# Splitting both products of an MLP into three one-pass products in a fused graph-transformer layer

## The chip, the cores and the metric

The kernel runs on one core of one Trainium2 chip. The metric is the device time of one execution, in microseconds (us). TensorE is called PE below, VectorE is DVE, ScalarE is ACT, GpSimd is POOL and SyncE is SP, as in the profile.

## The reference, cut to what matters

There are 6250 nodes with 512 features and 100000 edges. Three branches are computed and added up:

```python
xn = layernorm(x)
x = x + gnn(xn, edge_index, W1, b1, W2, b2) + mix(xn, ...)
x = x + ffn(layernorm(x))
# gnn: h = relu(xn @ W1 + b1) @ W2 + b2;  h + segment_sum(h[col], row)
# the end of mix:
y = v + (y @ proj_w + proj_b)
h2 = layernorm(y, n2_g, n2_b)
h2 = gelu(h2 @ mlp_w1 + mlp_b1)
h2 = h2 @ mlp_w2 + mlp_b2
return y + h2
```

The two products with `mlp_w1` and `mlp_w2` (both 512x512) are the ones that change.

## The kernel before

The 6250 rows are 125 partitions of 50 rows; a step handles two of the 50, so there are 25 steps (`STEPS`), numbered `t.u` from 0 to 24. The program has five stages, and every engine's order is written out by hand:

1. Start and first pass (`phase1`): weights are prepared, the edges are sorted on DVE, and the 256 hidden values of the gnn are stored to `hidden_rows` in HBM.
2. Second pass (`phase2`): the attention output of each step is computed and stored to `y_rows`. It has 8 edge groups in each step.
3. The mlp stage (`v` from 0 to 24 of the last loop): each step loads its `y_rows`, normalizes them on ACT (`norm_rows`, L1303), transposes them on PE (L973), multiplies by `mlp1_w` (`features`, L986, in two halves `i`), takes the gelu on ACT (`gelus`, L1331), multiplies by `mlp2_w` (`mlp2`, L995, in two halves), adds the result up on DVE (`z_rows`, L1881) and stores it to `z_rows` in HBM. It has 7 or 8 edge groups in each step, spread over it in four parts (`counts`).
4. The tail (`v` from 25 on, 3 edge groups a step while there are any left): the last branch (ffn) for each step, and the stores of the output.

Edge groups run under stages 2 to 4. There are 440 of them (`PAIRS`). A group is a pair of blocks of 128 edges. POOL issues one indirect DMA (a gather, L612) for each block, 880 in all, which brings the hidden rows of 128 edges into one place of a ring of 12 pairs (`RING`). ACT makes one-hot matrices for them (L1279, L1283), PE multiplies one by the other (L879 to L882), and DVE adds the sum to the accumulators in SBUF (`add_groups`, L1744). A gather for pair n waits until PE has used pair n - 12. PE's group n waits until both gathers of n have landed and until DVE has added group n - 2.

POOL's order in the last loop is: gathers up to a fixed number, then `roots` (L621, the inverse roots of the variances for the tail), then the next gathers. For `v` = 24 that is all gathers up to pair 405, which is gather 812, and then `roots` of step 0:

```python
gathers(TURN + sum(SECOND) + BETWEEN + sum(THIRD[:v]) + soon + RING)
if 0 <= b + 1 < STEPS:
    roots(steps[b + 1])
```

DVE's `ll_rows` (L1923) waits for these roots; behind it on DVE are the last `add_groups`, `z_rows` of step 24, and all of the tail.

SP's queue stores and loads in program order. In the mlp stage it stores `z_rows` of step v - 1, waits for that store, loads x for step v + 1, and then loads `y_rows` for step v + 2.

An f32 matmul is recorded as two matmuls by the profiler. Products with operands of type F32R are recorded as one each (L904 to L906 in `phase2`, for example), and so are those of 16 bit operands (L879 to L882).

## Time and profile before

| what | value |
| --- | --- |
| time, 3 runs | 1731.53 us median (1728.9 to 1735.38) |
| the profiled execution's own time | 1733.09 us |
| its span, first to last instruction | 1731.3 us |
| PE busy | 1598.6 us (92%) |
| DVE busy | 1044.2 us (60%) |
| ACT busy | 809.6 us (47%) |
| POOL busy | 1038.0 us (60%) |
| mean granted TensorE clock | 0.969 of full speed |

The profile gives each engine's busy time and, for each group of instructions, the idle time ahead of it and what ended that idle time. A share of busy time is an average over stages that have different limits, and it counts neither the sequencer's work between two instructions nor the waits. The second pass lasts from about 500 to 1012 us, the mlp stage from there to about 1480 us, and the tail to the end.

### The profile page before, as it was taken

To read this page: it belongs to the slowest core of one execution; us is meant where nothing else is said; L and a number is where in the kernel's file an instruction comes from. 1 tells how busy PE (TensorE), PEld (TensorE's weight loads), DVE (VectorE), ACT (ScalarE), POOL (GpSimd) and SP (SyncE) were. 2 spreads that over 40 slices of the span, in tenths; PEclk is the share of its full clock that TensorE was granted. 3 is DMA by queue.
4 is the path that set the end of the run, shared out by engine and by line. 5 is a ranking of instruction groups with operands and counts; after the bars stand their busy time and mean duration, and the time that the engine had idled before them with its cause. 6 is when DMAs were issued, how large, how long until landed. Compare 5 with 4: busy or idle time off the path is not lost.

```text
span 1731.3 us, 25102 instructions
## 1 busy us (share of the span) xinstructions
PE 1598.6 (92%) x8243; PEld 1241.5 (72%) x8243; DVE 1044.2 (60%) x2340; ACT 809.6 (47%) x1892; POOL 1038.0 (60%) x1131
## 2 busy tenths in 40 slices
PE   5999999998899999999999889999999999689997
PEld 3778877787677788878888656777667667467775
DVE  6899999997245555556555433333334334478896
ACT  2234444444334444445445555554654555256543
POOL 3124444343667777777777777777777777767110
PEclk9999999999899999999999889999999999899998
DMA  6023232322346556555665565666556566545332
GB/s 197 13 69 120 87 99 81 103 74 83 118 122 202 176 173 190 184 178 176 182 190 181 167 205 175 183 187 186 186 181 188 188 182 192 176 143 184 139 130 100
DMA packets 87427, 263.63 MB, mean 152 GB/s; under 512 B 18765, under 2 KB 20813, under 8 KB 87298
## 3 DMA queue, kind: packets, MB, share of 16 engines
q0 software_dynamic: 43456, 119.44, 24.7%
q1 hardware_dynamic: 43842, 142.59, 23.9%
q8 instruction: 68, 1.11, 0.3%
q14 instruction: 61, 0.50, 0.1%
HBM read 217.15 MB, written 44.80 MB: 151 GB/s over the span
## 4 chain that ended last, share of the span: by engine, by line
PE 44%; DMA 16%; DVE 15%; issue 11%; POOL 8%; ACT 5%; DVEq 0%; SPq 0%; POOLq 0%; ACTq 0%
PE bank L995 7%; DMA sb_step<-y_rows 6%; DVE sb_weights L1464 6%; DMA z_rows<-sb_step 5%; POOL sb_weights L612 4%; PE bank L934 3%; PE bank L986 3%; PE bank L904 2%; PE bank L906 2%; PE bank L905 2%; DMA sb_step<-x_t 2%; PE turn_bank L880 2%; PE bank L880 2%; DMA sb_weights<-hidden_rows,sb_weights 2%; DVE sb_step L1645 2%
## 5 line engine op out<-in xcount | busy, mean ns | idle before, releaser
L612 POOL DMA_INDIRECT sb_weights<-hidden_rows,sb_weights x880 | 862.6, 980 | 291.1 <-issue 246.1
L1279 ACT ACTIVATE sb_weights<-sb_const,sb_weights 128x125 f16<-128x125 f16 x880 | 266.9, 393 | 46.7 <-PE turn_bank L882 46.7
L1744 DVE TENSOR_TENSOR sb_acc<-sb_acc,bank 125x257 f32 x220 | 92.4, 420 | 301.4 <-PE bank L882 256.8
L995 PE MATMUL bank<-sb_weights,sb_step 128*125 128x512 f32 x400 | 181.6, 597 | 2.3 <-ACT sb_step L1402 2.3
L986 PE MATMUL bank<-sb_weights,sb_step 128*128 128x250 f32 x800 | 179.2, 377 | 0.0
L1744 DVE TENSOR_TENSOR sb_acc<-sb_acc,turn_bank 125x257 f32 x220 | 92.3, 419 | 143.5 <-PE turn_bank L882 125.1
L1464 DVE TENSOR_TENSOR sb_weights<-sb_weights 128x512 f32<-128x512 f32 (+3 forms) x256 | 164.3, 683 | 3.6
L986 PEld LDWEIGHTS bank<-sb_weights,sb_step 128*128 128x128 f32 x800 | 149.5, 192 | 15.8
L579 POOL TENSOR_SCALAR sb_const<-sb_const 125x2 f32<-125x2 f32 x25 | 10.0, 402 | 239.8 <-ACT sb_step L1181 239.8
L1197 ACT ACTIVATE sb_step<-sb_step 125x256 f32<-125x256 f32 x100 | 48.1, 502 | 214.0 <-DVE sb_step L1637 213.4
L728 PE MATMUL bank<-sb_w_parts,sb_x_high 128*125 128x512 f32 (+1 forms) x400 | 139.3, 348 | 0.0
L729 PE MATMUL bank<-sb_w_parts,sb_x_high 128*125 128x512 f32 (+1 forms) x400 | 135.3, 338 | 0.0
L730 PE MATMUL bank<-sb_w_parts,sb_x_low 128*125 128x512 f32 (+1 forms) x400 | 135.1, 338 | 0.0
L995 PEld LDWEIGHTS bank<-sb_weights,sb_step 128*125 128x125 f32 x400 | 71.7, 189 | 76.3 <-issue 73.7
L1283 ACT ACTIVATE sb_weights<-sb_weights,sb_const 128x1000 f16<-128x1000 f16 x110 | 124.1, 1129 | 3.6
L1303 ACT ACTIVATE sb_step<-sb_step,sb_const 125x512 f32<-125x512 f32 x50 | 37.9, 805 | 182.6 <-DMA sb_step<-y_rows 181.8
L741 PE MATMUL bank<-sb_w_parts,sb_x_high 128*125 128x256 f32 (+1 forms) x300 | 102.5, 342 | 16.3 <-DVE sb_step L1645 13.6
L1317 ACT COPY sb_step<-bank 128x500 f32<-128x500 f32 x25 | 14.4, 576 | 192.5 <-PE bank L922 192.5
L934 PE MATMUL bank<-sb_const,sb_step 128*125 128x512 f32 x200 | 95.3, 599 | 0.0
L743 PE MATMUL bank<-sb_w_parts,sb_x_low 128*125 128x256 f32 (+1 forms) x300 | 94.6, 315 | 0.0
L742 PE MATMUL bank<-sb_w_parts,sb_x_high 128*125 128x256 f32 (+1 forms) x300 | 94.5, 315 | 0.0
L835 PE MATMUL bank<-sb_step 125*128 125x256 f32 x400 | 90.8, 380 | 1.1 <-ACT sb_step L1257 1.1
(314 smaller groups left out, 3654.5 us busy)
## 6 DMA issues: line engine op xcount, KB each, us to landing
sb_step<-x SPq DMA_DIRECT2D x63, 500.0 KB
sb_step<-x_t SPq DMA_DIRECT2D x50, 500.0 KB, 6.8
sb_weights<-hidden_rows,sb_weights POOLq DMA_INDIRECT x880, 4.6
y_rows<-sb_step SPq DMA_DIRECT2D x25, 500.0 KB
sb_step<-y_rows SPq DMA_DIRECT2D x25, 500.0 KB
z_rows<-sb_step SPq DMA_DIRECT2D x25, 500.0 KB
sb_step<-z_rows SPq DMA_DIRECT2D x13, 500.0 KB
out<-sb_step SPq DMA_DIRECT2D x13, 500.0 KB
```

The costliest lines, as they stand in the source:

```text
L612: pool.indirect_dma_start(out=ring[:, n % RING * 2 + h, 0:HID], out_offset=None, in_=table, in_offset=bass.IndirectOffsetOnAxis(ap=row_of[ ...
L728: pe.matmul(bk, high, rhs(0, c), start=c == 0, stop=False)
L729: pe.matmul(bk, high, rhs(1, c), start=False, stop=False)
L730: mm = pe.matmul(bk, low, rhs(0, c), start=False, stop=c == KC - 1)
L741: pe.matmul(outs[c], high, first, start=c == 0, stop=False)
L934: mm = pe.matmul(banks[m][0:P, :], qpT[:, c, m * P:(m + 1) * P], pmat[:, c, :], start=False, stop=c == KH - 1)
L986: last = pe.matmul(bk[:, (c % 2) * 250:(c % 2) * 250 + 2 * P], mlp1_w[:, k, c * 128:(c + 1) * 128], hT3[:, t.s, k, :], start=k == 0, stop= ...
L995: mm = pe.matmul((BC, BD)[m][0:P, :], gT3[:, k, m * P:(m + 1) * P], mlp2_w[:, k, :], start=k == 0, stop=k == KC - 1)
L1279: mm = act.activation(hit[q % 2][:, i, :], iota_h[:, :], ACT.Abs, bias=less_lane[:, q * BP + i // 2, i % 2:i % 2 + 1])
L1283: act.activation(hit[q % 2], hit[q % 2], ACT.Relu, scale=-1.0, bias=one_c[:, 0:1]).then_inc(hits, 1)
L1464: sort_op(dve.tensor_tensor(half(target, c, lo), a, b, op))
L1744: dve.tensor_tensor(dst, dst, (BE, BH)[n % 2][0:P, 0:RW], ALU.add).then_inc(g_add, 1)
```

## The change

`features` gets its weights and its activations as two f16 parts each. The weights are scaled by a power of two for each output column, and the gelu's `scale` on ACT takes the power back. `mlp2` gets both operands as two F32R parts. Each product then becomes high x high, high x low and low x high, three matmuls of one pass. What goes with it:

- In the second pass, DVE and PE find the columns' squared norms (`mlp1_square_rows` behind step 4, `mlp1_norms` and `mlp1_scales` behind step 5), turn the powers into a column per output (`mlp1_columns`, `mlp1_scaled` behind step 6) and split the weights (`mlp1_halves` behind step 7).
- The first load of `y_rows` (`load_yd(0, 0)`), which has taken place in SP's queue behind step 3, moves behind step 11.
- ACT writes the high part of the transposed rows (`copy_hT`) and DVE the low part (`hT_low`). DVE writes both parts of the gelus (`split_gelus`). `mlp2` now waits for DVE's `g_split` instead of ACT's `feat_c`.
- `mlp2_w` is split once, its high part on ACT and its low part on DVE in step 0 of the mlp stage.

```diff
+        G_WORDS, G_AT, G_HIGH_AT, W2_HIGH_AT = KC * 2 * P, 7072, 8632, 128
...
+        G_LOW = sb("gelus_low", G_WORDS)
+        sb("rows_behind_gelus", G_HIGH_AT - G_AT - G_WORDS)
+        G_HIGH = sb("gelus_high", G_WORDS)
+        sb("mlp1_place", STEP_WORDS + W2_HIGH_AT - G_HIGH_AT - G_WORDS)
+        W2_HIGH = sb("mlp2_high", KC * D)
+        sb("constants_behind", CONST_WORDS - W2_HIGH_AT - KC * D)
...
-        mlp2_w, (gnn2_w, gnn2_low), (_, gnn2_high) = same_place(KC, D)[0], same_place(KH, D), same_place(KH, D)
-        hT3, z_first = same_place(2, KC, 2 * P)[0], [same_place(2, D)[0] for _ in range(3)]
+        (mlp2_w, mlp2_low), (gnn2_w, gnn2_low), (_, gnn2_high) = same_place(KC, D), same_place(KH, D), same_place(KH, D)
+        mlp2_high = by_chunk(W2_HIGH[:, :])
+        hT_place, z_first = same_place(2 * KC * 2 * P)[0], [same_place(2, D)[0] for _ in range(3)]
+        hT3 = hT_place.bitcast(F16).rearrange("p (s h c r) -> p s h c r", s=2, h=2, c=KC)
...
+        halves_of = lambda v: [v[:, at:at + D // 2].bitcast(F16) for at in range(0, v.shape[1], D // 2)]
+        mlp1_squares = [ATT[:, RAW_WORDS + 2 * D:RAW_AT], EDGE[:, 4 * PAIRS:4 * PAIRS + D], halves[0][:, D:2 * D], halves[1][:, D:2 * D]]
+        mlp1_high = halves_of(EDGE[:, 4 * PAIRS:4 * PAIRS + 3 * D // 2]) + halves_of(mlp1_w[:, 0, :])[1:]
+        mlp1_low = [zero_row.bitcast(F16), halves_of(mlp1_w[:, 0, :])[0]] + halves_of(mlp1_w[:, 1, :])
+        mlp1_back = n2g
...
-                elif t.u == 3:
+                elif t.u == 11:
                     sp.wait_ge(r_st[0], 16 * 13 + 1)
                     sp.wait_ge(r_st[1], 16 * 12 + 1)
+                    sp.wait_ge(*made("mlp1_split"))
                     load_yd(0, 0)
...
+            def mlp1_norms():
+
+                pe.wait_ge(*made("mlp1_squares"))
+                for k in range(KC):
+                    mm = pe.matmul(BF[:, :], ones[:, :], mlp1_squares[k], start=k == 0, stop=k == KC - 1)
+                mm.then_inc(made("mlp1_norms")[0], 1)
+
+            def mlp1_columns():
+
+                pe.wait_ge(*made("mlp1_scales"))
+                for c in range(KC):
+                    mm = pe.matmul(BF[:, c:c + 1], mlp1_squares[0][0:1, c * 128:(c + 1) * 128], ones[0:1, 0:1], start=True, stop=True)
+                mm.then_inc(made("mlp1_columns")[0], 1)
...
                 if t.u == 4:
                     pe.wait_ge(ev("m1b_ok"), 1)
+                elif t.u == 6:
+                    pe.wait_ge(*made("mlp1_scales"))
+                elif t.u == 7:
+                    pe.wait_ge(*made("mlp1_columns_read"))
...
+                elif t.u == 5:
+                    mlp1_norms()
+                elif t.u == 6:
+                    mlp1_columns()
...
                     for k in range(KC):
-                        last = pe.matmul(bk[:, (c % 2) * 250:(c % 2) * 250 + 2 * P],
-                                         mlp1_w[:, k, c * 128:(c + 1) * 128], hT3[:, t.s, k, :],
-                                         start=k == 0, stop=k == KC - 1)
+                        high, low = (v[k][:, c * 128:(c + 1) * 128] for v in (mlp1_high, mlp1_low))
+                        pe.matmul(out, high, hT3[:, t.s, 0, k, :], start=k == 0, stop=False)
+                        pe.matmul(out, high, hT3[:, t.s, 1, k, :], start=False, stop=False)
+                        last = pe.matmul(out, low, hT3[:, t.s, 0, k, :], start=False, stop=k == KC - 1)
                 last.then_inc(feat, 1)
 
             def mlp2(t, i):
-                pe.wait_ge(feat_c, t.u * 2 + i + 2)
+                pe.wait_ge(g_split, t.u * 2 + i + 2)
                 for m in (0, 1):
                     for k in (2 * i, 2 * i + 1):
-                        mm = pe.matmul((BC, BD)[m][0:P, :], gT3[:, k, m * P:(m + 1) * P], mlp2_w[:, k, :],
-                                       start=k == 0, stop=k == KC - 1)
+                        high, low = (v[:, k, m * P:(m + 1) * P].bitcast(F32R) for v in (g_high, g_low))
+                        w_high, w_low = (v[:, k, :].bitcast(F32R) for v in (mlp2_high, mlp2_low))
+                        pe.matmul((BC, BD)[m][0:P, :], high, w_high, start=k == 0, stop=False)
+                        pe.matmul((BC, BD)[m][0:P, :], high, w_low, start=False, stop=False)
+                        mm = pe.matmul((BC, BD)[m][0:P, :], low, w_high, start=False, stop=k == KC - 1)
...
-            def copy_hT(t, dst):
+            def copy_hT(t):
 
                 for i, bk in ((0, BF), (1, BG)):
                     act.wait_ge(tr, t.g * 2 + i + 2)
-                    act.copy(dst[:, t.s, 2 * i:2 * i + 2, :].rearrange("p a b -> p (a b)"), bk[:, 0:500]).then_inc(h_t, 1)
+                    act.copy(hT3[:, t.s, 0, 2 * i:2 * i + 2, :].rearrange("p a b -> p (a b)"), bk[:, 0:500]).then_inc(hT_high, 1)
...
-                                        bias=m1b[:, c:c + 1])
+                                        scale=mlp1_back[:, c:c + 1], bias=m1b[:, c:c + 1])
...
             act.wait_ge(ev("m1b_ok"), 1)
+            act.wait_ge(w2m_in, 16)
+            act.wait_ge(y_read, 2 * STEPS + 1)
+            act.copy(mlp2_high.bitcast(F32R), mlp2_w).then_inc(made("mlp2_high")[0], 1)
...
+            def mlp1_square_rows():
+
+                for k in range(KC):
+                    mm = dve.tensor_tensor(mlp1_squares[k], mlp1_w[:, k, :], mlp1_w[:, k, :], ALU.mult)
+                mm.then_inc(made("mlp1_squares")[0], 1)
+
+            def mlp1_scales():
+
+                dve.wait_ge(*made("mlp1_norms"))
+                back, scale, bits, _ = (v.bitcast(I32) for v in mlp1_squares)
+                seq(dve.tensor_copy(mlp1_squares[2], BF[:, :]))
+                ts(bits, bits, 24, ALU.logical_shift_right)
+                ts(scale, bits, -1.0, ALU.mult, 203.0, ALU.add)
+                ts(bits, bits, 51.0, ALU.add)
+                ts(scale, scale, 23, ALU.logical_shift_left)
+                ts(back, bits, 23, ALU.logical_shift_left)
+                dve.drain().then_inc(made("mlp1_scales")[0], 1)
+
+            def mlp1_scaled():
+
+                dve.wait_ge(*made("mlp1_columns"))
+                dve.tensor_copy(mlp1_back[:, :], BF[:, 0:KC])
+                dve.drain().then_inc(made("mlp1_columns_read")[0], 1)
+                seq(dve.tensor_tensor(mlp1_w, mlp1_w, mlp1_squares[1].unsqueeze(1).to_broadcast([128, KC, D]), ALU.mult))
+
+            def mlp1_halves():
+
+                for k in range(KC):
+                    if k < 3:
+                        seq(dve.tensor_copy(mlp1_high[k], mlp1_w[:, k, :]))
+                    seq(dve.tensor_tensor(mlp1_low[k], mlp1_w[:, k, :], mlp1_high[k], ALU.subtract))
+                    if k == 0:
+                        seq(dve.tensor_copy(mlp1_high[3], mlp1_w[:, 3, :]))
+                dve.drain().then_inc(made("mlp1_split")[0], 1)
...
+                elif t.u == 4:
+                    mlp1_square_rows()
+                elif t.u == 5:
+                    mlp1_scales()
+                elif t.u == 6:
+                    mlp1_scaled()
+                elif t.u == 7:
+                    mlp1_halves()
...
+            def hT_low(t):
+
+                for i, bk in ((0, BF), (1, BG)):
+                    part = lambda h: hT3[:, t.s, h, 2 * i:2 * i + 2, :].rearrange("p a b -> p (a b)")
+                    dve.wait_ge(hT_high, t.g * 2 + i + 2)
+                    dve.tensor_tensor(part(1), bk[:, 0:500], part(0), ALU.subtract).then_inc(h_t, 1)
+            hT_low(each_step(0)[0])
...
+            def split_mlp2():
+
+                dve.wait_ge(*made("mlp2_high"))
+                dve.tensor_tensor(mlp2_low.bitcast(F32R), mlp2_w, mlp2_high, ALU.subtract).then_inc(made("mlp2_split")[0], 1)
+
+            def split_gelus(t, i):
+
+                part = lambda v: v[:, 2 * i:2 * i + 2, :].rearrange("p a b -> p (a b)")
+                dve.wait_ge(feat_c, t.u * 2 + i + 2)
+                seq(dve.tensor_copy(part(g_high).bitcast(F32R), part(gT3)))
+                dve.tensor_tensor(part(g_low).bitcast(F32R), part(gT3), part(g_high), ALU.subtract).then_inc(g_split, 1)
...
-                    add_groups(counts[0] + counts[1])
+                    add_groups(counts[0])
+                    if a == 0:
+                        split_mlp2()
+                    split_gelus(steps[a], 0)
+                    add_groups(counts[1])
+                    split_gelus(steps[a], 1)
+                    if a + 1 < STEPS:
+                        hT_low(steps[a + 1])
```

What stands on DVE in one step of the mlp stage. Before, from the step's addition of y and x (L1871, L1873) on, with the adds of two groups (L1744, each behind its register load, ISA):

```order
L1871 TENSOR_TENSOR sb_step<-sb_step 125x1024
L1873 TENSOR_TENSOR sb_step<-sb_step,sb_const 125x1024
L1744 ISA
L1744 TENSOR_TENSOR sb_acc<-sb_acc,bank 125x257
L1744 ISA
L1744 TENSOR_TENSOR sb_acc<-sb_acc,turn_bank 125x257
```

Now, in the changed kernel, from the second of these adds on (L1794 there):

```order
L1794 TENSOR_TENSOR sb_acc<-sb_acc,turn_bank 125x257
L1985 CAST sb_gelus_high<-sb_step 128x500
L1986 TENSOR_TENSOR sb_gelus_low<-sb_step,sb_gelus_high 128x500
L1794 ISA
L1794 TENSOR_TENSOR sb_acc<-sb_acc,bank 125x257
L1794 ISA
L1794 TENSOR_TENSOR sb_acc<-sb_acc,turn_bank 125x257
L1985 CAST sb_gelus_high<-sb_step 128x500
L1986 TENSOR_TENSOR sb_gelus_low<-sb_step,sb_gelus_high 128x500
L1948 TENSOR_TENSOR sb_weights<-bank,sb_weights 128x500
L1948 TENSOR_TENSOR sb_weights<-turn_bank,sb_weights 128x500
```

Each step gains a cast and a subtraction from SBUF for each half of the gelus, and two subtractions from PSUM for the next step's transposed rows.

What stands on DVE between step 5 and step 6 of the second pass. Before, the end of `row_stats` (L1771) and the start of the next step:

```order
L1769 BN_AGGR sb_const<-sb_const 125x2 x2
L1771 COPY sb_const<-sb_const 125x4
L1814 SCALAR_TENSOR_TENSOR sb_step<-sb_step,sb_const 125x256 x2
L1818 TENSOR_SCALAR sb_step<-sb_step 125x2
L1820 RECIPROCAL sb_step<-sb_step 125x2
```

Now, in the changed kernel, the same place (L1821 is the end of `row_stats`, L1899 the start of step 6):

```order
L1819 BN_AGGR sb_const<-sb_const 125x2 x2
L1821 COPY sb_const<-sb_const 125x4
L1869 COPY sb_step<-bank 128x512
L1473 TENSOR_SCALAR sb_step<-sb_step 128x512
L1473 TENSOR_SCALAR sb_weights<-sb_step 128x512
L1473 TENSOR_SCALAR sb_step<-sb_step 128x512
L1473 TENSOR_SCALAR sb_weights<-sb_weights 128x512
L1473 TENSOR_SCALAR sb_weights<-sb_step 128x512
L1899 SCALAR_TENSOR_TENSOR sb_step<-sb_step,sb_const 125x256 x2
```

`mlp1_scales` has come in between: a read of PSUM and five operations on 512 columns, behind a wait for PE.

What stands on PE between the same two steps. Before, the last product of y (L934), the last group and the first product of the next step (L904):

```order
L934 MATMUL bank<-sb_const,sb_step 125x512 x2
L879 MATMUL turn_bank<-sb_weights 125x257
L880 MATMUL turn_bank<-sb_weights 125x256 x2
L882 MATMUL turn_bank<-sb_weights 125x257
L904 MATMUL bank<-sb_w_parts,sb_x_high 125x512
```

Now, in the changed kernel:

```order
L972 MATMUL bank<-sb_const,sb_step 125x512 x2
L899 MATMUL turn_bank<-sb_weights 125x257
L900 MATMUL turn_bank<-sb_weights 125x256 x2
L902 MATMUL turn_bank<-sb_weights 125x257
L920 MATMUL bank<-sb_weights,sb_const 128x512 x2
L920 MATMUL bank<-sb_step,sb_const 128x512 x2
L938 MATMUL bank<-sb_w_parts,sb_x_high 125x512
```

`mlp1_norms` has come in: four f32 products of 512 columns.

## Rows read from the trace of the kernel before

**Rows 1.** Groups by line, 1012 to 1465 us: count, busy us, mean ns, idle before:

```profile
L612 POOL DMA_INDIRECT sb_weights<-hidden_rows,sb_weights x355 | 345.2, 972 | 108.2 <-issue 98.1 <-PE turn_bank L882 6.1 <-PE bank L882 4.0
L995 PE MATMUL bank<-sb_weights,sb_step 128*125 128x512 f32 x384 | 174.4, 597 | 2.3 <-ACT sb_step L1402 2.3
L986 PE MATMUL bank<-sb_weights,sb_step 128*128 128x250 f32 x768 | 172.1, 377 | 0.0
...
L1871 DVE TENSOR_TENSOR sb_step<-sb_step 125x1024 f32<-125x1024 f32 x24 | 29.4, 1227 | 3.1 <-DMA sb_step<-x 2.5 <-DVE sb_const L1862 0.2
...
L1858 DVE TENSOR_SCALAR sb_weights<-sb_weights,sb_const 128x512 f32<-128x512 f32 x2 | 0.9, 478 | 0.0
```

**Rows 2.** The chain that ended last, in order: start us, us, what:

```profile
1260.78 12.35 DMA z_rows<-sb_step
1273.53 14.31 DMA sb_step<-y_rows
1290.51 3.44 PE bank L995 x8
...
1299.68 12.34 DMA z_rows<-sb_step
```

**Rows 3.** Groups by line from the start to 607.0 us, POOL, then PE:

```profile
L612 POOL DMA_INDIRECT sb_weights<-hidden_rows,sb_weights x120 | 119.2, 994 | 50.1 <-issue 34.7 <-DMA hidden_rows<-sb_step 6.7 <-PE bank L882 6.7
L879 PE MATMUL bank<-sb_weights 128*125 128x257 f16 x25 | 7.2, 288 | 8.2 <-DMA sb_weights<-hidden_rows,sb_weights 6.5 <-DVE sb_acc L1744 1.7
```

**Rows 4.** The same from the start to 1471.2 us:

```profile
L612 POOL DMA_INDIRECT sb_weights<-hidden_rows,sb_weights x794 | 777.4, 979 | 257.1 <-issue 223.0 <-PE bank L882 14.9 <-PE turn_bank L882 12.5
L879 PE MATMUL bank<-sb_weights 128*125 128x257 f16 x196 | 54.6, 278 | 16.9 <-DMA sb_weights<-hidden_rows,sb_weights 7.2 <-issue 4.8 <-DVE sb_acc L1744 4.6
```

**Rows 5.** Timeline of POOL: start us, us, what, idle before:

```profile
607.54 0.94 POOL L612 DMA_INDIRECT sb_weights<-hidden_rows,sb_weights  x1 [1.17 <-PE bank L882]
...
627.25 0.96 POOL L612 DMA_INDIRECT sb_weights<-hidden_rows,sb_weights  x1 [0.30 <-issue]
...
646.69 1.04 POOL L612 DMA_INDIRECT sb_weights<-hidden_rows,sb_weights  x1 [0.30 <-issue]
...
1224.64 1.82 POOL L612 DMA_INDIRECT sb_weights<-hidden_rows,sb_weights  x1 [0.30 <-issue]
...
1493.60 0.95 POOL L612 DMA_INDIRECT sb_weights<-hidden_rows,sb_weights  x1 [0.30 <-issue]
1494.57 0.72 POOL L621 TENSOR_TENSOR sb_step<-sb_step,sb_const 125x2 f32<-125x2 f32 x1
```

**Rows 6.** Timeline of DVE, columns as in rows 5:

```profile
627.38 0.62 DVE L1827 TENSOR_SCALAR sb_step<-sb_step 125x256 f32<-125x256 f32 x2
...
646.55 0.62 DVE L1827 TENSOR_SCALAR sb_step<-sb_step 125x256 f32<-125x256 f32 x2
...
1224.41 1.22 DVE L1871 TENSOR_TENSOR sb_step<-sb_step 125x1024 f32<-125x1024 f32 x1
...
1495.33 0.16 DVE L1923 SCALAR_TENSOR_TENSOR sb_step<-sb_step 125x2 f32<-125x2 f32 x1 [14.25 <-POOL sb_step L621]
```

**Rows 7.** Timeline of PE, two F32R and two f16 products:

```profile
607.57 0.40 PE L906 MATMUL bank<-sb_w_parts,sb_x_low 128*125 128x512 f32 x1
607.80 0.40 PE L904 MATMUL bank<-sb_w_parts,sb_x_high 128*125 128x512 f32 x1
...
1211.21 0.27 PE L879 MATMUL bank<-sb_weights 128*125 128x257 f16 x1
1211.32 0.38 PE L880 MATMUL bank<-sb_weights 128*125 128x256 f16 x2
```

**Rows 8.** The chain that ended last, at step 4 of the second pass:

```profile
586.64 10.13 DMA sb_step<-x_t
```

**Rows 9.** DMA issues of the page, KB each, median us to landing:

```profile
sb_step<-x_t SPq DMA_DIRECT2D x50, 500.0 KB, 6.8
sb_weights<-hidden_rows,sb_weights POOLq DMA_INDIRECT x880, 4.6
```

More of the change, by code:

```diff
@@ L1367, in _ @@
             act.wait_ge(v_mm, STEPS + 1)
-            copy_hT(steps[0], hT3)
+            copy_hT(steps[0])
             one_hots(2 * STEPS + 4)
@@ L1387, in _ @@
                     if a + 1 < STEPS:
-                        copy_hT(steps[a + 1], hT3)
+                        copy_hT(steps[a + 1])
                     hits_until(ahead + sum(counts[0:2 if a == 2 else 3]))
```

34 lines of the change are left out of this document (20 added, 14 removed).

## The prediction

> **What bounds the kernel now.** I began with the chain of waits, since PE is busy for 92% of the span. In the mlp stage the chain runs through PE's products and, every two steps, through a store of z_rows (12.35 us) and a load of y_rows (14.31 us); from one such store to the next it is 1299.68 - 1260.78 = 38.9 us, 19.4 a step [rows 2]. Read alone, this says that the mlp's products set the time. So the next view is that of the groups by line in this stage, and there the row to look at is POOL's, which the chain hardly names. Of 453 us the gathers fill 345.2 us busy and 108.2 us idle, which is all of it, and the idle time is 108.2 / 355 = 0.30 us ahead of each [rows 1]. A single gather shows the same 0.30 us, named "issue" [rows 5]: that is POOL's own time between two of them, not a wait. POOL is thus full at one gather per 1.25 us or a little more (0.95 + 0.30), whatever its 60% of busy time says.
>
> Does PE wait for it? A count tells. By 1471.2 us POOL has begun 794 gathers and PE 196 + 196 pairs (the row of the other bank has the same count), that is 784 gathers [rows 4]. The lead is 10 gathers, 12.5 us, and 4.6 us of it are the landing [rows 9]. So PE could be about 8 us ahead of where it is, once, and no more. At 607.0 us it was otherwise: 120 gathers begun, 25 + 24 pairs used, a lead of 22 of the 24 places of the ring [rows 3], and POOL had to wait for a place (1.17 us instead of 0.30 us at 607.54 [rows 5]; there are four such waits from 584 to 611 us, of 1.96, 1.04, 1.17 and 1.04 us). So up to about 611 us PE holds POOL back, and from there on POOL is the one that never stops.
>
> The end of this is the third thing to see. POOL's roots for step 0 of the tail stand behind gather 812. It ends at 1494.55 us and the roots start at 1494.57 [rows 5]; DVE had waited for them for 14.25 us [rows 6], and all of the tail stands behind this. The gathers therefore set the time up to 1494.6 us, and the 236.7 us behind that are the tail, in which the change has no instruction. What makes the mlp stage shorter on PE ends in a longer wait at this place.
>
> **The change on PE.** F32R products of 512 columns follow each other at 607.80 - 607.57 = 0.23 us, and f16 ones of 257 at 1211.32 - 1211.21 = 0.11 us [rows 7]. A step of the mlp stage has 16 x 3 f16 products of 250 columns, 48 x 0.107 = 5.1 us, in place of 172.1 / 24 = 7.2 us, and 8 x 3 F32R products, 24 x 0.233 = 5.6 us, in place of 174.4 / 24 = 7.3 us busy [rows 1]; by start times it is 3.44 us for four products, 6.9 us a step [rows 2], and the like for the others, 6.8. PE's work falls by 13.7 - 10.7 = 3.0 us a step, 72 us over 24 steps. I count 0 for it, because the gathers cover it. If they did not, it would be -72.
>
> **The second pass.** `mlp1_norms` is four f32 products of 512 columns, 3.44 us [rows 2], on PE behind step 5. POOL has hardly any slack there: at pair 68, whose place PE frees just behind, it issues 1 us later than it could. Alone this would cost 3.44 - 1.0 = 2.4 us. But the load of y_rows that moves away from step 3 stood ahead of the x_t load of step 4, which took 10.13 us [rows 8] against 6.8 us in the median [rows 9]; PE then stood still for 2.2 us and ran 2 us more at the 1.2 GHz level, so that step 4 took 23.5 us where the next took 19.3. Without it PE is 4.1 us earlier, more than the norms take, and two of the four waits of POOL (0.87 + 0.74 us over 0.30) go. I take -1.6 us, with +2.4 as the other end. At step 11 the load gives the 4 us back, but there POOL has 8 us of slack in the ring. DVE gets 2 to 5 us more behind each of the steps 4 to 7; the longest, eight casts and subtractions of 512 columns behind step 7, makes its first add some 5 us late and PE some 2.4 us, when POOL has 4 us of slack. Cost 0; with less slack up to 2 us.
>
> **What DVE does to the gathers.** This is the term that is left. The gather at 1224.64 took 1.82 us and not 0.95. It started 0.23 us into DVE's L1871, an addition with both inputs in SBUF, which ran until 1225.63. What was left of L1871 were 0.99 us, and the excess is 0.87 us, 0.1 us less [rows 5, 6]. The one at 646.69 started 0.14 us into the first of two L1827, a one-input operation of 0.35 us, so 0.21 us before its end, and took 1.04, 0.09 us more; the one at 627.25 started 0.13 us ahead of the same L1827 and took 0.96 [rows 5, 6]. So a DVE operation of effective length d (its duration less 0.1) delays a gather that starts inside it, to its end, and no other. With gathers every 1.25 us the expected delay is d x d / 2.5 for short ones. For L1871, 24 times with d = 1.1, that is 11.6 us; measured is 355 x (972 - 947) ns = 8.9 us over the stage [rows 1], 0.77 of it (0.947 us is an undisturbed gather). DVE's second addition right behind comes too soon after to hit another.
>
> New in each step are twice a cast of 500 columns (0.478 us for 512 of one input [rows 1], d = 0.35) and a subtraction of 500 with both inputs in SBUF (half of 1.227 us [rows 1] and a little, d = 0.57). (0.12 + 0.33) / 2.5 = 0.18 us each time, 0.36 a step, 8.6 us over 24 steps, times 0.77 = 7 us. Bounds: 2 us if they mostly fall beside the starts, 13 us if each delays one gather by a third of its length. `hT_low` has one input in PSUM, as the adds L1744, which delay nothing. Once each: two operations of 2048 columns with both inputs in SBUF (twice 1.227 us each, some 2.4), where a gather always starts and waits 2.3 - 0.6 = 1.7 us, 3.4 us; four squares, five integer operations and eight parts of 512 columns, together some 1.4 us. Times 0.77 it is 4 us (2 to 6).
>
> A rule of the Trainium skill speaks for more. SBUF — State Buffer, Two separate sides, says that while DVE runs a two-port operation, which an fp32 copy within SBUF is, GpSimd "cannot write the descriptors" of its DMAs. By that a cast would delay every gather that it touches, not only one that starts inside, and the time would be 1758 us (the third rival has it from rows). This trace does not agree: the gather at 627.25 was touched and not delayed.
>
> **The sum.** -1.6 + 4 + 7 = +9.4 us on a span of 1731.3, so 1740.7. The profiled execution's own time was 1.8 us more than its span and 1.6 us above the median of the three runs, so against the median I forecast 1731.5 + 9.4 = 1741 us.
>
> **The rivals.**
> - **PE is the bound after all**, as the chain has it: then the 3.0 us a step come through, less the links that DVE adds, 1731 - 72 = 1660 us, up to 1715 if only part does. For it: PE's 92%. Against it: a lead of only 10 gathers, and DVE's 14.25 us of wait. A chance of 0.07. It decides if gathers come faster than one per 1.25 us, or if the roots no longer wait for them.
> - **Nothing to see.** The casts and subtractions fall beside the gathers' starts (DVE now often runs just behind a landing, and so at a fixed place between two gathers), and POOL's waits at 584 to 611 us shrink: -1.6 + 2 + 2 = +2, 1734 us. Chance 0.24.
> - **Each cast delays each gather that it touches** (what the page says of two-port operations): 48 casts of 0.478 us [rows 1], a gather busy for 0.95 of 1.25 us, 0.4 us each, 19 us on top of the subtractions' 5 and the 4: 1758 us. For it: nothing in the rows; against it: 627.25. Chance 0.07.
> - **The loop through z_rows and y_rows takes over.** `mlp2` now waits for a cast and a subtraction on DVE behind the gelu (some 1.3 us, twice in two steps) and gets two halves that are 0.6 us shorter. The 38.9 us [rows 2] grow by about 1 us, 12 us in 24 steps, and PE enters the stage some 5 us later than before. DVE had 14.25 us in hand [rows 6] and gets 9 more; so it costs nothing unless the loop grows by 2 us or more. Then 1750 us. Chance 0.08.
> - **As forecast:** 1741 us, between 1736 and 1749, 0.54.
>
> **How the numbers follow.** A measurement of this kernel can tell about 0.5% from no change, 8.7 us. The forecast lies just above it at 1740.2, so its 0.54 I divide into 0.34 slower and 0.20 same; with the two slower rivals that is 0.49 slower, with the second 0.44 same, and 0.07 faster. For 8 in 10 the range goes from 1731 (nothing to see, with waits gone) to 1756.
>
> **What would show it.** In the profile after: PE's features and mlp2 together at about 10.7 us a step, and PE waiting for gathers or for norm_rows; the gathers still at 0.30 us idle, with a mean of about 990 ns in the mlp stage; the roots right behind gather 812, some 9 us later than 1494.6, with DVE's wait for them over 10 us; a tail of 237 us. I would be wrong if the gathers' mean stays at 972 ns, if POOL shows waits for PE behind 620 us, or if the tail changes its length, which none of my terms covers.

## The result: half a per cent slower, as forecast

The changed kernel took 1742.36 us in the median of 6 runs (1737.27 to 1745.26), the kernel before 1732.15 us (6 runs). The ratio is 1.0052, with a 95% interval of 1.0034 to 1.0071: slower by 10 us, at the edge of what can be told. The forecast was 1741 us. The profiled execution took 1745.26 us, with a span of 1743.4 us, 12.1 us more than the one of before. Each trace is one execution; single executions of the changed kernel differ by up to 8 us. This matters below.

The page of the changed kernel, its first lines and its chain:

```profile
span 1743.4 us, 26514 instructions
PE 1548.1 (89%) x8859; PEld 1254.1 (72%) x8859; DVE 1139.9 (65%) x2511; ACT 824.1 (47%) x1893; POOL 1048.8 (60%) x1131
...
POOL sb_weights L632 9%; DVE sb_weights L1514 6%; PE bank L972 4%; DMA sb_step<-y_rows 4%; DMA sb_weights<-hidden_rows,sb_weights 4%; DMA z_rows<-sb_step 3%; PE bank L938 3%; PE bank L939 3%; PE bank L940 3%; PE bank L1106 2%; PE bank L749 2%; PE bank L748 2%; PE turn_bank L900 2%; PE bank L750 2%; PE bank L900 2%
```

The gathers, line 632 now, lead the chain with 9% of the span; before they had 4%, and the chain hardly named them in the mlp stage. Now the groups by line in the changed kernel, 1012 to 1465 us, the same 453 us as in [rows 1]:

```profile
L632 POOL DMA_INDIRECT sb_weights<-hidden_rows,sb_weights x348 | 347.7, 999 | 106.0 <-issue 99.9 <-PE turn_bank L902 3.7 <-PE bank L902 2.4
...
L1041 PE MATMUL bank<-sb_mlp_high,sb_gelus_high 128*125 128x512 f32 x184 | 78.9, 429 | 9.6 <-DVE sb_gelus_low L1986 6.6 <-ACT sb_step L1452 3.0
```

Again busy and idle time of the gathers fill the 453 us, with 0.30 us ahead of each, but 7 fewer fit in, because the mean is 999 ns and not 972. PE's new products are as short as they should be. PE's timeline, two neighbours of each kind:

```profile
1180.26 0.39 PE L1043 MATMUL bank<-sb_mlp_high,sb_gelus_low 128*125 128x512 f32 x1
1180.49 0.39 PE L1041 MATMUL bank<-sb_mlp_high,sb_gelus_high 128*125 128x512 f32 x1
...
1188.68 0.27 PE L1030 MATMUL bank<-sb_weights 128*128 128x250 f16 x1
...
1189.00 0.27 PE L1030 MATMUL bank<-sb_weights 128*128 128x250 f16 x1
```

0.23 us for an F32R product, and three f16 ones in 0.32 us: 24 x 0.23 + 48 x 0.107 = 10.7 us a step. What PE saves it waits. Its longest waits in this stage, 1012 to 1478 us (us in total, times, longest):

```profile
PE turn_bank L899 <- DMA sb_weights<-hidden_rows,sb_weights: 38.8, 36, 2.2
PE bank L899 <- DMA sb_weights<-hidden_rows,sb_weights: 15.7, 11, 4.6
```

Last the timeline of POOL, at the places that matter:

```profile
776.27 0.95 POOL L632 DMA_INDIRECT sb_weights<-hidden_rows,sb_weights  x1 [1.38 <-PE bank L902]
...
779.51 0.94 POOL L632 DMA_INDIRECT sb_weights<-hidden_rows,sb_weights  x1 [1.04 <-PE turn_bank L902]
...
1284.68 1.99 POOL L632 DMA_INDIRECT sb_weights<-hidden_rows,sb_weights  x1 [0.30 <-issue]
...
1290.74 1.02 POOL L632 DMA_INDIRECT sb_weights<-hidden_rows,sb_weights  x1 [0.30 <-issue]
...
1294.58 0.94 POOL L632 DMA_INDIRECT sb_weights<-hidden_rows,sb_weights  x1 [0.30 <-issue]
...
1505.39 0.95 POOL L632 DMA_INDIRECT sb_weights<-hidden_rows,sb_weights  x1 [0.30 <-issue]
1506.37 0.72 POOL L641 TENSOR_TENSOR sb_step<-sb_step,sb_const 125x2 f32<-125x2 f32 x1
```

and of DVE:

```profile
1284.63 1.22 DVE L1971 TENSOR_TENSOR sb_step<-sb_step 125x1024 f32<-125x1024 f32 x1
...
1290.52 0.42 DVE L1985 CAST sb_gelus_high<-sb_step 128x500 fp32r<-128x500 f32 x1 [1.32 <-ACT sb_step L1378]
...
1294.66 0.68 DVE L1986 TENSOR_TENSOR sb_gelus_low<-sb_step,sb_gelus_high 128x500 fp32r<-128x500 f32 x1
...
1507.12 0.16 DVE L2035 SCALAR_TENSOR_TENSOR sb_step<-sb_step 125x2 f32<-125x2 f32 x1 [12.88 <-POOL sb_step L641]
```

Read the last rows first: the roots start at 1506.37, right behind gather 812, 11.8 us later than in [rows 5], and what is behind them takes 237.0 us, as before. DVE had waited 12.88 us. Then the cast: the gather at 1290.74 begins 0.22 us into it and takes 0.07 us too long. The subtraction at 1294.66 lies wholly within the gather at 1294.58 and delays it by nothing; it isn't delayed either, and takes the 0.68 us that it takes elsewhere. The worst is an old operation: the gather at 1284.68 began 0.05 us into the z_rows addition (L1971, L1871 before) and took 1.04 us too long.

### The profile page after: what moved, and what is told of

Its sections match the earlier page's. It is cut to its first block, busy times and chain, and to the rows that moved or that the text cites. A ratio compares the mean times of both kernels' runs of the same rounds, so it can differ in the third digit from the quotient of the medians.

```text
span 1743.4 us, 26514 instructions
## 1 busy us (share of the span) xinstructions
PE 1548.1 (89%) x8859; PEld 1254.1 (72%) x8859; DVE 1139.9 (65%) x2511; ACT 824.1 (47%) x1893; POOL 1048.8 (60%) x1131
## 4 chain that ended last, share of the span: by engine, by line
PE 45%; DVE 16%; DMA 13%; POOL 12%; issue 8%; ACT 6%; DVEq 0%; SPq 0%; POOLq 0%; ACTq 0%
POOL sb_weights L632 9%; DVE sb_weights L1514 6%; PE bank L972 4%; DMA sb_step<-y_rows 4%; DMA sb_weights<-hidden_rows,sb_weights 4%; DMA z_rows<-sb_step 3%; PE bank L938 3%; PE bank L939 3%; PE bank L940 3%; PE bank L1106 2%; PE bank L749 2%; PE bank L748 2%; PE turn_bank L900 2%; PE bank L750 2%; PE bank L900 2%
## 5 line engine op out<-in xcount | busy, mean ns | idle before, releaser
L632 POOL DMA_INDIRECT sb_weights<-hidden_rows,sb_weights x880 | 874.1, 993 | 290.7 <-issue 247.2
L1794 DVE TENSOR_TENSOR sb_acc<-sb_acc,bank 125x257 f32 x220 | 92.5, 420 | 202.0 <-PE bank L902 163.4
L1794 DVE TENSOR_TENSOR sb_acc<-sb_acc,turn_bank 125x257 f32 x220 | 92.4, 420 | 116.1 <-PE turn_bank L902 103.4
L899 PE MATMUL bank<-sb_weights 128*125 128x257 f16 x220 | 62.1, 282 | 55.3 <-DMA sb_weights<-hidden_rows,sb_weights 20.4
L899 PE MATMUL turn_bank<-sb_weights 128*125 128x257 f16 x220 | 63.8, 290 | 52.4 <-DMA sb_weights<-hidden_rows,sb_weights 41.7
L1041 PE MATMUL bank<-sb_mlp_high,sb_gelus_high 128*125 128x512 f32 x200 | 85.8, 429 | 10.0 <-DVE sb_gelus_low L1986 7.0
L900 PE MATMUL turn_bank<-sb_weights 128*125 128x256 f16 x440 | 86.7, 280 | 0.0
```

The lines of the kernel that those rows point to most:

```text
L632: pool.indirect_dma_start(out=ring[:, n % RING * 2 + h, 0:HID], out_offset=None, in_=table, in_offset=bass.IndirectOffsetOnAxis(ap=row_of[ ...
L899: pe.matmul(bk[0:P, 0:RW], one_hot, row[:, LOW_AND_ONE], start=True, stop=False)
L900: mm = pe.matmul(bk[0:P, 0:HID], one_hot, row[:, HIGH], start=False, stop=False)
L1794: dve.tensor_tensor(dst, dst, (BE, BH)[n % 2][0:P, 0:RW], ALU.add).then_inc(g_add, 1)
```

## The experiments

Four kernels ran on a first chip, where the kernel before took 1898.67 us (18 runs). The other eight ran on chips where it took about 1734 us, nearly as in the case itself. Ratios are to the kernel before on the same chip.

**Half of the mlp's products, in the kernel before.** It asks the main question, whether PE's time is worth anything.

```diff
-                    for k in range(KC):
+                    for k in range(2):
...
-                                         start=k == 0, stop=k == KC - 1)
+                                         start=k == 0, stop=k == 1)
...
-                    for k in (2 * i, 2 * i + 1):
+                    for k in (2 * i,):
...
-                                       start=k == 0, stop=k == KC - 1)
+                                       start=k == 0, stop=k == 2)
```

> The kernel before with half of the mlp stage's products left out (the features sum over two of four chunks, mlp2 over one of two in each half), so the output is another. PE has about 6.8 us a step less, 163 us over 24 steps. If the gathers are the bound, as I say: no change, 1732 us within 3, roots(0) at 1494 to 1496 us, gathers still at 0.30 us idle, and PE's idle time up by 150 us or more. If PE is the bound: 70 to 160 us less, 1570 to 1660.

On the first chip: 1891.19 us, a ratio of 0.9952 (0.9933 to 0.9971), 7.5 us less for some 160 us of PE's work. So it was run again on a chip of the usual speed:

> The same kernel as e2_before_half_mlp, once more, for the same reason (half of the mlp stage's products are left out of the kernel before, so the output is another). If the gathers are the bound: within 3 us of the kernel before, since each gather still takes 1.25 us, and PE's idle time up by 130 us or more. What could come back beyond that: the first chip gave 7.5 us. If PE is the bound where gathers are faster: 70 to 160 us less.

1734.39 us (10 runs) against 1734.09, a ratio of 1.0002 (0.9989 to 1.0015). Its groups by line, 1012 to 1465 us:

```profile
L612 POOL DMA_INDIRECT sb_weights<-hidden_rows,sb_weights x353 | 345.9, 980 | 107.6 <-issue 99.7 <-PE turn_bank L882 4.0 <-PE bank L882 4.0
```

PE's waits in that stretch:

```profile
PE turn_bank L879 <- DMA sb_weights<-hidden_rows,sb_weights: 76.5, 47, 4.0
PE bank L879 <- DMA sb_weights<-hidden_rows,sb_weights: 20.9, 19, 3.7
```

and the end of the stretch on POOL:

```profile
1497.09 0.95 POOL L612 DMA_INDIRECT sb_weights<-hidden_rows,sb_weights  x1 [0.30 <-issue]
1498.06 0.74 POOL L621 TENSOR_TENSOR sb_step<-sb_step,sb_const 125x2 f32<-125x2 f32 x1
```

Half of the products are gone, PE waits 97 us for gathers in these two rows, and neither the number of gathers in 453 us (353, before 355) nor the roots nor the end come earlier. PE's busy time in the stretch fell by 108 us (436.7 to 328.9), less than the 130 us expected, since the granted clock was 0.89 there and 0.99 before. The rival "PE is the bound after all" is out, by a run and not by argument. The roots at 1498.06, 3.5 us later than in [rows 5], are within what executions differ by.

**Without the casts and subtractions, and with the casts alone.**

```diff
-                seq(dve.tensor_copy(part(g_high).bitcast(F32R), part(gT3)))
-                dve.tensor_tensor(part(g_low).bitcast(F32R), part(gT3), part(g_high), ALU.subtract).then_inc(g_split, 1)
+                if t.u == 0:       # not in the kernel with the casts alone
+                    seq(dve.tensor_copy(part(g_high).bitcast(F32R), part(gT3)))
+                wide = 2
+                dve.tensor_tensor(part(g_low)[:, 0:wide].bitcast(F32R), part(gT3)[:, 0:wide], part(g_high)[:, 0:wide], ALU.subtract).then_inc(g_split, 1)
```

In both, `mlp2` reads the high part in place of the low one.

> The changed kernel without DVE's casts and subtractions behind the gelus: the cast is made at the first step only, the subtraction is cut to 2 columns, and PE reads the high part in place of the low one, so the output is another. PE has the same products. My theory (a gather that starts inside one of these operations is delayed to its end): 7 us less than the changed kernel, between 2 and 13, so 1735 us, and roots(0) some 7 us earlier, again right behind gather 812. If the delay of the gathers has another source (PE's products, the order of the loads, or the loop through z_rows and y_rows that waits for these operations), 1742 with the same mean of a gather in the mlp stage; if the loop is the cause, the gathers' mean stays and DVE's wait for the roots grows. If each cast delays each gather that it touches: 20 us or more less, 1722.

> The changed kernel with DVE's casts behind the gelus kept and the subtractions cut to 2 columns; PE reads the high part in place of the low one, so the output is another. My theory, by which a delay grows with the square of an operation's length: the subtractions are 4.8 of the 7 us and the casts 1.8, so 1737.5 us here, 2 us above the kernel without both. If a copy within SBUF delays each gather that it touches, nearly all of the cost stays: 1741 or more.

1908.61 and 1908.79 us, ratios of 1.0050 (1.0030 to 1.0069) and 1.0048 (1.0030 to 1.0066): nothing between them. But this chip has another bound. The timeline of POOL in the first of the two:

```profile
1394.95 0.95 POOL L632 DMA_INDIRECT sb_weights<-hidden_rows,sb_weights  x1 [0.30 <-issue]
1398.09 0.95 POOL L632 DMA_INDIRECT sb_weights<-hidden_rows,sb_weights  x1 [2.19 <-remote]
1399.35 0.94 POOL L632 DMA_INDIRECT sb_weights<-hidden_rows,sb_weights  x1 [0.30 <-issue]
```

About every tenth gather there (29 of 304 from 1012 to 1465 us) waits some 2 us for something that the trace names "remote", and they come one per 1.49 us in the mean. A delay by DVE could disappear within such a wait; no run shows that it does. Something else stands out in PE's waits, 1160 to 1225 us:

```profile
PE bank L1041 <- ACT sb_step L1452: 6.9, 1, 6.9
```

That is PE at an early `mlp2` of the stage, waiting once for ACT to empty a bank with a product for the tail. The change didn't bring it in: the kernel before has the same wait (L1402, 2.3 us in [rows 1]), and the changed kernel on a usual chip has it with 3.0 us. Here it is longer, and POOL then stood 8.05 us for a place in the ring (7.8 and 9.8 us in the two other variants of the changed kernel that ran on this chip, 3.2 us in the kernel before with half of the products). In the changed kernel's trace of the usual speed POOL has no wait there. So these variants, 0.5% slower here too, may be so for another reason; it is not shown, since no run takes this wait away and the changed kernel itself did not run on this chip. The two runs therefore decide nothing. The kernel without both was run again on a chip of the usual speed:

> The same kernel as e1_no_gelu_parts, once more, because the chip of that run had another bound: its gathers had a wait of some 2 us at every eighth to tenth, so that one came per 1.46 us, and a delay by DVE was hidden in these waits. On a chip where the kernel before takes about 1733 us: by my theory 7 us less than the changed kernel (2 to 13), a ratio to before of 1.001 to 1.002 in place of 1.005, gathers of the mlp stage at a mean of 975 to 980 ns. If the delay of the gathers has another source: a ratio of 1.005 here too. On a chip like the first, it says nothing new.

1741.04 us (7 runs), a ratio of 1.0046 (1.0029 to 1.0064), where 1.001 to 1.002 was expected and the changed kernel has 1.0052. Yet its trace shows what was expected; the groups, 1012 to 1465 us:

```profile
L632 POOL DMA_INDIRECT sb_weights<-hidden_rows,sb_weights x355 | 345.2, 972 | 108.2 <-issue 100.9 <-PE turn_bank L902 4.3 <-PE bank L902 3.0
```

That is the row of the kernel before again. The execution of this trace took 1731.81 us, the fastest of the seven, and the other six took 1737.31 to 1744.40. A single trace speaks for its own execution only, and this one doesn't stand for the kernel.

**The same operations made twice**, the opposite test:

```diff
+                seq(dve.tensor_copy(part(g_high).bitcast(F32R), part(gT3)))
+                seq(dve.tensor_tensor(part(g_high).bitcast(F32R), part(gT3), part(g_high), ALU.subtract))
                 seq(dve.tensor_copy(part(g_high).bitcast(F32R), part(gT3)))
                 dve.tensor_tensor(part(g_low).bitcast(F32R), ...).then_inc(g_split, 1)
```

> The changed kernel with the cast and the subtraction behind each half of the gelus made twice on DVE (the first pair into the high part's place, then the pair itself), 96 more operations of 500 columns within SBUF. The same outputs. My theory in the size that the traces so far give (the mlp stage is 4 us shorter without these operations, the forecast said 7): a second set costs 4 to 7 us more than the changed kernel, 1746 to 1749 us on a chip where before takes 1733, a ratio of 1.008 to 1.009. If these operations cost the time nothing, as the timed runs of the kernel without them say (1.0046 beside 1.0052): 1742 us, 1.005. If the loop through z_rows and y_rows is near its end, which gets 1.4 us longer twice a step: over 1755 us.

1745.56 us (6 runs), a ratio of 1.0063 (1.0048 to 1.0077), just below the 1746 to 1749 us of the expectation, and in its trace, 1012 to 1465 us:

```profile
L632 POOL DMA_INDIRECT sb_weights<-hidden_rows,sb_weights x350 | 347.4, 993 | 106.6 <-issue 99.6 <-PE turn_bank L902 4.0 <-PE bank L902 3.0
```

Without, once, twice: 1.0046, 1.0052, 1.0063, each against the kernel before on its own chip. The two sets together are worth 0.0017, 3 us, so one is worth 1.5 us. By the intervals of the two ends (0.0018 and 0.0015, together 0.0023) it is between nothing and some 3.5 us. The 7 us of the forecast are excluded if sets add up, but the 2 us that it had as the lower bound are not. Whether sets add up is not shown.

**The gelus in PSUM.**

```diff
-                    mm = act.activation(gT3[:, c, :], (BA, BB)[i][:, ...], ACT.Gelu,
+                    at = (BA, BB)[i][:, (c % 2) * 250:(c % 2) * 250 + 250]
+                    mm = act.activation(at, at, ACT.Gelu,
...
-                pe.wait_ge(feat_c, max(1, t.g * 2 + i))
+                pe.wait_ge(g_split, max(1, t.g * 2 + i))
...
-                seq(dve.tensor_copy(part(g_high).bitcast(F32R), part(gT3)))
+                gelu = (BA, BB)[i][:, 0:500]
+                seq(dve.tensor_copy(part(g_high).bitcast(F32R), gelu))
```

(and the subtraction and PE's wait ahead of the tail in the same way).

> The changed kernel with the gelus written back into their PSUM bank and not to SBUF, so that cast and subtraction each read them from PSUM; the next features wait for the subtraction. No DVE operation of the pair has two inputs in SBUF, and the cast has none. My theory: these operations then delay no gather, as the adds with an input in PSUM, and 5 to 7 us go, 1735 to 1737 us. If what counts is only how long DVE is busy, or if the next features come late by the longer hold of the bank: 1742 us or a little more.

1911.35 us on the first chip, 1.0055 (1.0035 to 1.0074), where 5 to 7 us less was expected: no help, on a chip that decides nothing here. It stands again in the last kernel below, on a chip of the usual speed.

**The load of y_rows at step 11.**

```diff
                     load_x2(Step(2, t.u + 2))
+                if t.u == 11:
+                    ...
+                    load_yd(0, 0)
                 if t.u < STEPS - 1:
                     store_y(t)
...
-                elif t.u == 11:
-                    ...
-                    load_yd(0, 0)
```

The load now stands behind the loads of x_t and x of its own step and ahead of the store of y_rows, no longer right ahead of the next step's load of x_t. In time it goes earlier. SP's queue in the changed kernel, and the load that matters in its chain of waits:

```profile
748.24 0.26 SPq L468 DMA_DIRECT2D sb_step<-y_rows  x1
751.17 0.36 SPq L420 DMA_DIRECT2D sb_step<-x_t  x1
...
751.17 14.13 DMA sb_step<-x_t
```

and SP's queue with the load moved:

```profile
734.10 0.41 SPq L468 DMA_DIRECT2D sb_step<-y_rows  x1
...
752.41 0.36 SPq L420 DMA_DIRECT2D sb_step<-x_t  x1
```

> The changed kernel with the load of y_rows at step 11 put behind the load of x_t on SP's queue and not ahead of it; nothing else. The trace of the changed kernel shows 8 us lost by PE there (the x_t load took 14.1 us) and two waits of POOL for a place in the ring, of 1.4 and 1.0 us in place of 0.3. My theory, that this is a part of what the change cost: 1.8 to 2.4 us less, 1740.3 us, and neither wait. If POOL's lead in the ring makes it up: the same 1742.

1740.94 us (5 runs), 1.0045 (1.0028 to 1.0061). In its POOL timeline, to be held against the waits at 776.27 and 779.51 of the changed kernel:

```profile
776.48 0.94 POOL L632 DMA_INDIRECT sb_weights<-hidden_rows,sb_weights  x1 [0.30 <-issue]
...
778.99 0.94 POOL L632 DMA_INDIRECT sb_weights<-hidden_rows,sb_weights  x1 [0.30 <-issue]
```

The waits are gone, and the x_t load takes 7.9 us. Their price, 1.38 + 1.04 - 0.60 = 1.8 us, is too small for the timed runs to show (1.4 us less than the changed kernel, and uncertain by more than that). The slow load is there in all four traces with the old order (13.7 to 14.8 us), and each time it makes PE's step 8.2 to 9.5 us longer than the 19.3 us of its neighbours. Whether POOL then waits depends on its lead: it did in three of the four, by 1.6 to 4.1 us, and not in the changed kernel with the roots 8 pairs earlier, where it had stood 4.92 us for a place at 586.2 us.

**The roots ahead of some gathers.** If the tail stands behind roots(0) and these behind gather 812, they could go first.

```diff
-                gathers(TURN + sum(SECOND) + BETWEEN + sum(THIRD[:v]) + soon + RING)
+                ahead = TURN + sum(SECOND) + BETWEEN + sum(THIRD[:v]) + soon + RING
+                gathers(ahead if b + 1 != 0 else ahead - 8)
```

> The kernel before with POOL's roots for step 0 of the tail put ahead of the last 16 gathers that run ahead of them. The variances were there at 1478.3 us, the roots started at 1494.6. If what stands ahead of the tail is POOL's row of gathers and nothing else: roots at about 1479 us, 14 us less, 1718 us. If the gathers behind the roots are late for their pairs by then, PE waits for them and less comes back: 1724 or more. If DVE or PE would have been late anyway: 1732.

> The changed kernel with the same move of the roots, 16 gathers earlier. The variances were there at 1489.6 us, the roots started at 1506.4. My theory: roots at about 1490 us and 14 to 16 us less, 1727 us, with the tail at 237 us. If PE now waits for the last gathers: 1735. The mlp stage of the changed kernel has a variance later than before by as much as the gathers are late, so the gain is the same as in the kernel before, and not greater, if PE's shorter products are worth nothing at this place; greater by 5 us or more if they are worth something.

1734.55 us (10 runs), 1.0002 (0.9991 to 1.0014), and, in the changed kernel, 1744.22 us (6 runs), 1.0068 (1.0051 to 1.0085). My 14 us were wrong in both. POOL's timeline, from the kernel before with this move:

```profile
1478.06 0.94 POOL L612 DMA_INDIRECT sb_weights<-hidden_rows,sb_weights  x1 [0.30 <-issue]
1483.41 0.72 POOL L621 TENSOR_TENSOR sb_step<-sb_step,sb_const 125x2 f32<-125x2 f32 x1 [4.41 <-DVE sb_step L1918]
```

POOL stops 4.41 us for the variances, and pays for that with all gathers behind. The other half of the answer is in the kernel before without the move, one step of the tail later:

```profile
1509.38 0.95 POOL L612 DMA_INDIRECT sb_weights<-hidden_rows,sb_weights  x1 [0.30 <-issue]
1514.16 0.72 POOL L621 TENSOR_TENSOR sb_step<-sb_step,sb_const 125x2 f32<-125x2 f32 x1 [3.83 <-DVE sb_step L1917]
```

Roots(1) waited for DVE for only 3.83 us. Behind them the row of gathers takes over again, and no order can bring more than about this and the waits that follow from it. So the move was made smaller, 3 pairs in place of 8 (`ahead - 3`):

> The kernel before with the roots of step 0 of the tail 6 gathers earlier, and not 16. Read from the traces: with 16, POOL stood 4.4 us at the roots, because the variances were not there yet, and then the roots of step 1 came right behind gather 823, with no wait; in the kernel before they came 3.8 us after that gather, waiting for DVE. So two paths meet at the roots of step 1: the gathers up to 823, and roots 0 and the 19.6 us from them to roots 1. With 6 gathers earlier roots 0 start at about 1487 us, without a wait, the second path ends at 1507 and the first sets roots 1 at 1511 in place of 1514.2: 3 to 4 us less, 1730 us. If the order at this place is worth nothing: the same time.

1728.52 us (10 runs) against 1733.94: 0.9975 (0.9963 to 0.9987), 4.3 to 5.4 us less by ratio and medians, and **faster than both kernels**. POOL's timeline:

```profile
1486.90 0.95 POOL L612 DMA_INDIRECT sb_weights<-hidden_rows,sb_weights  x1 [0.30 <-issue]
1487.88 0.72 POOL L621 TENSOR_TENSOR sb_step<-sb_step,sb_const 125x2 f32<-125x2 f32 x1
...
1510.53 0.95 POOL L612 DMA_INDIRECT sb_weights<-hidden_rows,sb_weights  x1 [0.30 <-issue]
1511.49 0.74 POOL L621 TENSOR_TENSOR sb_step<-sb_step,sb_const 125x2 f32<-125x2 f32 x1
```

Neither of the roots waits any more.

**All three** (the gelus in PSUM, the load moved, the roots 8 pairs earlier) on the changed kernel:

> The changed kernel with all three: the gelus written back into PSUM, the load of y_rows behind that of x_t at step 11, and the roots 16 gathers earlier. My theory adds the parts, 6 + 2 + 15 us: 1719 us, less than both kernels. If the roots alone count and the gathers' time is hidden behind them: as with the early roots alone, 1727.

1738.74 us (12 runs), 1.0033 (1.0019 to 1.0048), not 1719. Against the early roots alone, on the same chip, it is 0.0035 less, 6 us, with an interval of about 0.0012 to 0.0058. How it divides between the load and the gelus no run shows; neither trace has a wait of POOL for a place just behind step 11. In the traces the gathers 449 to 812 took 12.6 us over 0.95 us each with the early roots alone and 10.1 us here, 2.5 us less. Its gathers, 1012 to 1465 us:

```profile
L632 POOL DMA_INDIRECT sb_weights<-hidden_rows,sb_weights x353 | 346.2, 981 | 107.6 <-issue 101.2 <-PE turn_bank L903 4.0 <-PE bank L903 2.4
```

## Why the prediction was right, and where its terms were off

**PE's shorter products count 0: shown.** With half of the products left out, more than the change saves, the ratio is 1.0002.

**The roots stand behind gather 812, and the tail is 237 us: read again** in the changed kernel. In the three other traces with the changed code and the roots in their old place the tail is 234.1 to 234.8 us, so it isn't quite fixed. The prediction's sentence that all of the tail stands behind these roots was too strong. Two paths meet again one step later, at roots(1), 3.8 us apart (3.6 us in the changed kernel); a delay of the gathers comes through nearly whole, because it moves both, while an advance of the roots alone is worth 4 to 5 us.

**The second pass, -1.6 us, and the once-only operations, +4 us.** Their sum was +2.4; from the first gather to the 449th, ahead of nearly all of the mlp stage, it took 585.8 us before (443.8 to 1029.6) and 589.3 us in the changed kernel (444.6 to 1033.9). Over all traces from chips of the usual speed, four with the code of before in this stretch and five with that of the changed kernel (a load apart, or with fewer gelu parts, which come last in it), the difference is 4.5 us in the mean: 3.5 us of it are longer gathers, about the 4 us of the forecast for the once-only operations, and 1.0 us longer waits, where it had -1.6. Two of the waits for a place were gone, as forecast, but others came, of 0.48 and 0.82 us just behind the norms (627.8 and 631.0 us) and behind step 11. The step that failed is the one on step 11: "the load gives the 4 us back, but there POOL has 8 us of slack in the ring". There PE lost some 8 us, not 4, because the x_t load, issued 2.9 us behind that of y_rows, took 14.1 us to land, and PE's products then came 0.43 us apart and not 0.23, with the granted clock at its 1.2 GHz level for 6.8 us from 767.6 us on; and POOL waited, 1.8 us in all. Moving the load took these waits away. That the prediction named waits behind 620 us as a sign against it was right, at a price of 2 us.

**The casts and subtractions, +7 us: the mechanism stands, the size does not.** A gather is delayed only if it starts inside the operation, to that one's end less some 0.1 us, as the rows at 1290.74 and 1294.58 show for both cases. Counted over the trace of the changed kernel (gathers that start inside and take over 0.97 us), the 100 delay 22 gathers by 2.5 us in all, in the kernel with all three (inputs in PSUM) none. With random starts I had 9 us (less by 0.77). Where the sum went wrong is the assumption that starts are random and independent. A subtraction stands right behind its cast, like L1871's second addition, for which the prediction had said this itself. The starts show it: of the 21 gathers that start inside a subtraction, five do so 0.01 to 0.03 us behind its start and are not delayed at all, and the other 16 start 0.36 us or more into it and lose at most 0.19 us each. None starts in between, where random starts would put 13 of 50 and the delay is longest; nor does one in three other traces. Why not, no run shows. The timed runs give 1.5 us for one set, between 0 and 3.5.

**What the forecast did not have: the old addition hits more often.** Counted in the same way, the 25 z_rows additions delay 16 gathers by 8.7 us in the trace of before and 24 gathers by 13.7 us in that of the changed kernel. It is the same operation at other places between two gathers. It explains more of the mean of 999 ns than the new operations do, and it varies: 8.7 to 11.3 us in the four traces with the code of before, 10.2 to 13.7 in the four with the new operations read from SBUF, 7.4 and 9.1 in the two without. Whether the changed kernel shifts these places for good, or the execution fell so, is not settled by so few traces.

**What stays open.** The terms that are shown add up to 4.5 + 1.5 = 6 us, and the medians differ by 10. The traces by themselves come nearer: over the gathers 449 to 812 the excess over 0.95 us each is 9.6 us in the mean of the four traces with the code of before (8.6 to 11.0) and 14.8 us in the three with one set of the new operations (12.6 to 16.1), 5.2 us more, of which about half are the z_rows additions; with the 4.5 us that is 9.7. But the timed runs of the kernel without the new operations do not bear this out. Most puzzling, the kernel without the gelu parts should be at 1737 us, and is at 1741.04 while its one trace says 1731.81. Its executions are spread more than most: this kernel and two other variants of the changed one take 12.6 to 13.3 us from the fastest to the slowest in 6 to 12 runs, the changed kernel itself and two more variants 5.0 to 8.0 us in 5 or 6, and the kernel before 5.0 to 9.5 us in 15 to 23. What spreads them is not in the traces that there are. That the total came out within 1.4 us of the forecast is thus partly luck: one term too small by 2 us, one too large by some 5, and some 4 us that no term had.

**The rivals.** PE as the bound: out. The loop through z_rows and y_rows: out, since DVE still waits 12.88 us for the roots, and a second set of these operations in the loop costs 2 to 3 us (by the intervals at most some 6) and leaves DVE a wait of 10.45 us. Each cast delays each gather that it touches: out, by the gather at 1294.58, which a subtraction lay within, and by 50 more casts for 2 to 3 us with their subtractions. By the Trainium skill (SBUF — State Buffer, Two separate sides), GpSimd cannot write descriptors while such an operation runs; but the same section adds that whoever starts first gets the shared ports and blocks the other, which the third rival left out. The trace agrees for a gather that begins in an operation (1290.74), and for one under way (1294.58), which isn't delayed. It does not agree that the operation which comes second is blocked: the subtraction at 1294.66 took its usual 0.68 us.

## What to carry to other kernels

An engine with 60% of busy time can be the bound, and one with 92% can be free: count how many instructions of each had begun at two moments, and add busy and idle time in a stretch to see whether an engine ever stops for another. Before work is moved ahead of a queue on the bounding engine, look at the next place where the two paths meet, and move by no more than the waits there allow (3 pairs gave 4 to 5 us, 8 pairs nothing). A sum of small collisions needs several executions or a test of none, one and two sets: a single trace had the right mechanism here and a size that the timed runs did not bear out.

## What was not expected of the hardware

- One chip took 1898.67 us for the kernel that takes 1734 us on others. In the traces from it a gather in about ten waits some 2 us ("remote"), and half of the mlp's products are worth 7.5 us there and nothing on the others.
- DVE operations within SBUF do not delay a gather under way (0.94 us for the one at 1294.58), and those that read PSUM delay none: of the 53 gathers that start in one of the 100 in the kernel with all three, none takes over 0.97 us.
- Two loads of 500 KB issued 2.9 us apart: the second took 14.1 us to land, where the median is 6.5 us, and 13.7 to 14.8 us in all four traces with this order.
